# Weight casts issued ahead of group 0's masks, half transposes ahead of the context stores, the down tile's load behind a denominator hop

## The chip, the cores and the metric

The kernel runs on one core of one Trainium2 chip. The metric is the device time of one execution in microseconds (us), lower is better; the time before is the median of three runs.

## The reference

Two transformer layers over x of shape 1 x 1024 x 512. The part around the change is the first layer's attention and the weights that the later parts need:

```python
q = jnp.dot(x, Wq)                  # 32 query heads of 16
k, v = ...                          # 8 key/value heads; 4 query heads share one
scores = einsum('bhqd,bhkd->bhqk', q, k); scores = where(causal, -inf, scores)
ctx = softmax(scores / sqrt(16)) @ v
x = x + layernorm(ctx @ Wo + bo)
# L0 ffn: gate_t, up_t, down_t are int32 in {-1, 0, 1}, scaled by row
hidden = silu(x @ gate_w.T) * (x @ up_w.T); out = hidden @ down_w.T
# L1: mixing along D by autocorrelation (rfft, top 6 lags, softmax, rolled sums)
# L1 ffn: the same form with float weights w plus low-rank terms, w + b @ a
```

Every sublayer ends in a layernorm and a residual sum.

## The kernel before, in words

The program is written engine by engine, with semaphores set by hand; the order of each engine's work is the order of the code.

**Ahead of attention.** The projections are made and split in three bf16 pieces, which go out to `qp_d` and `kp_d` in DRAM. Beside them the low-rank products `b @ a` of the second ffn are made tile by tile (L1108), copied by ACT (L929), added by POOL to the loaded weight tile (`pool_lora`, L1050, 22 tiles) and stored by ACT's queue (L919).

**Attention in eight groups of four heads** (`for_groups`: group 0, a loop over groups 1 to 4, then groups 5, 6, 7 written out). For the eight key tiles kt of a group g, PE makes: row scores of a group ahead (L1533, plus the diagonal's mask L1536), of which DVE takes row maxima (L1418, L1420); transposed scores of g (L1546), which ACT exponentiates (L1506) and POOL masks on the diagonal (L1398); and the weighted sums (L1569). The row scores run `NT + LEAD` = 14 tiles ahead: from kt = 2 of group g they are those of group g + 2. Their queries lie in `qt6`, a ring of three, so the queries of group g + 2 may be loaded only when group g - 1 has used its own: `sp_group` waits for `st_ready` and then issues `load_q(sp, g + 2)` (L1307, six DMAs of 128 KB) at the very start of group g.

**SyncE's queue (SP)** issues nearly every DMA, in program order, and stands still at each wait. One group before the change: the queries' load; the down tile's load (L442, 688 KB, groups 1 to 4); then seven hops in the order of `HOPS`: "den" of the group before (denominators out L1328, back as 128 x 32 L1331, reciprocals out L1334, broadcast back L1338) and "max" of the next group (transpose L1314, out L1317, back L1320); then the context stores (L1346, four DMAs, which wait until POOL has normalised in L1389), the down tile's store (L447, which waits for DVE's sum L1131) and, in groups 1 to 4, `sp_weights0`: one DMA transpose of half of a weight (L432 for up, L434 for down). Group 0 is followed by the transpose of the whole gate weight (L432) and by `sp_early`, three small loads (L389 to L391).

**The casts.** gate_t, up_t and down_t are int32 in DRAM. Three DMAs of POOL's queue write them to DRAM as 16-bit numbers (`w16_d`); the gate's is issued near the start (L1676), those of up and down (L1407, L1408) at the end of POOL's part of group 0, behind its eight masks. `sp_weights0` waits for them (`w0_cast`).

The rest (output product, first ffn, mixing, second ffn) begins behind group 7 and is not touched.

Of the kernel before, what the change touches and what calls it, by code (L numbers as in the profile page):

```python
# [97 lines left out]
def build(nc, x_in, Wq, Wkv, Wo, bo, gate_t, up_t, down_t, gate_s, up_s, down_s,  # L98
          gate_w, up_w, down_w_in, gate_a, gate_b, up_a, up_b, down_a, down_b, dft, power, inverse, out):
    with ExitStack() as ctx:  # L100
# [337 lines left out]
        def down_row_load(sp, n):  # L438

            if n > 0:  # L440
                sp.wait_ge(down_stored, 16 * n)
            sp.dma_start(down_w, down_lora_w[n * P:(n + 1) * P, :]).then_inc(down_loaded, 16)  # L442
# [846 lines left out]
        def for_groups(eng, body):  # L1289

            body(eng, 0, 0)
            with eng.Fori(1, ND + 1) as g:
                body(eng, g, 1)
            body(eng, ND + 1, ND + 1)
            body(eng, G - 2, G - 2)
            body(eng, G - 1, G - 1)
# [48 lines left out]
                at = REP * HD * upper + HD * h  # L1345
                sp.dma_start(ctxt[at:at + HD, g - ND * upper, :], ctxn[32 * h:32 * h + HD, :]).then_inc(stored or ctx_stored, 16)  # L1346

        def sp_group(sp, g, shape, upper=0, w0=None):


            if shape < G - 2:

                if shape > 0:
                    sp.wait_ge(st_ready, 32 * g)
                else:
                    sp.wait_ge(qt_loaded, 2 * 16 * len(TERMS))
                load_q(sp, g + 2)
            if 1 <= g <= ND:
                down_row_load(sp, g - 1)
            for path, hop in HOPS:  # L1360
                if path == "den" and shape > 0:
                    den_hop(sp, g - 1, hop)
                if path == "max" and shape < G - 1:
                    maxima_hop(sp, g + 1, hop)
                if shape == G - 1 and (path, hop) == ("den", 1):
                    hidden_store(sp, 1, 5)
            if shape == G - 2:
                sp.wait_ge(st_ready, 32 * (G - 2))
                hidden_load(sp, 2)
                hidden_load(sp, 3)  # L1370
            if shape == G - 1:
                hidden_store(sp, 2, 6)
            if shape > 0:
                ctx_store(sp, g - 1, upper)
            if 1 <= g <= ND:
                down_row_store(sp, g - 1)
            if shape == G - 2:
                hidden_store(sp, 0, 4)
            if shape == G - 1:
                hidden_store(sp, 3, 7)  # L1380
            if w0 is not None:
                sp_weights0(sp, w0)

        def normalise(pool, g):

            pool.wait_ge(rec_loaded, 16 * REP * (g + 1))
# [4 lines left out]
        def pool_group(pool, g, shape):  # L1391

            for kt in range(NT):
                pool.wait_ge(p_ready, 32 * g + 4 * kt + 4)
                diag = probs[:, kt % 2, :, kt * P:(kt + 1) * P]
                pool.sem_inc(pool_passed)

                nc.gpsimd.affine_select(out=diag, in_=diag, compare_op=ALU.is_ge, fill=0.0, base=0,  # L1398
                                        pattern=[[0, REP], [1, P]], channel_multiplier=-1).then_inc(masked, 1)
                if kt == 0:  # L1400
                    if shape > 0:
                        pool.wait_ge(pv_done, NT * g)
                    nc.gpsimd.tensor_copy(vcur[:, :, 0:HD], vall[:, :, g, :]).then_inc(vcur_ready, 1)
                if kt == NORM_STEP and shape > 0:
                    normalise(pool, g - 1)
            if shape == 0:
                pool.dma_start(w16_d[1], up_t).then_inc(w0_cast[1], 16)  # L1407
                pool.dma_start(w16_d[2], down_t).then_inc(w0_cast[2], 16)  # L1408

        def row_max(dve, g, pos, before=None):  # L1410

# [189 lines left out]
        @block.sync  # L1601
        def _(sp):
            for half in range(2):
                sp.dma_start(x[:, 4 * half:4 * half + 4, :], x_in[0].rearrange("(t p) d -> p t d", p=P)[:, 4 * half:4 * half + 4, :]).then_inc(x_loaded[half], 16)
            sp.wait_ge(lora_clear, 1)
            sp_lora(sp)
            sp.dma_start(wkv, Wkv.rearrange("(c p) n -> p c n", p=P)).then_inc(wkv_loaded, 16)
            sp.dma_start(wq, Wq.rearrange("(c p) n -> p c n", p=P)).then_inc(wq_loaded, 16)
            sp_lora_stack(sp)

            for j in range(1 + ND):
                sp.wait_ge(pieces_ready, j + 1)
                for i in range(3):
                    dst = kp_d[i] if j == 0 else qp_d[i, (j - 1) * P:j * P, :]
                    sp.dma_start(dst, pc[i][:, j % 2, :]).then_inc(pieces_stored[j % 2], 16)
                if j == 0:
                    sp_lora_rows(sp)
                    sp.wait_ge(pieces_stored[0], 48)
                    for _, s, n in BLOCKS:
                        sp.dma_start(kt6[HD * s:HD * (s + n), :, :].rearrange("p g t -> p (g t)"),  # L1620
                                     kp_d[0:n].rearrange("a (d g) t -> (a d) (g t)", g=G)).then_inc(kt_loaded, 16)
                if j == 1:
                    sp.wait_ge(pieces_stored[1], 48)
                    load_q(sp, 0)
                    sp.wait_ge(qt_loaded, 16 * len(TERMS))
                    load_q(sp, 1)
            sp_lora_down(sp)
            for upper in range(2):
                half = slice(upper * D // 2, (upper + 1) * D // 2)
                sp.dma_start(wo[upper * P // 2:(upper + 1) * P // 2, :, :],  # L1630
                             Wo[half, :].rearrange("(c p) n -> p c n", p=P // 2)).then_inc(wo_loaded, 16)
            sp.wait_ge(pieces_stored[0], 48 * 3)
            sp.wait_ge(pieces_stored[1], 48 * 2)
            for hop in range(3):
                maxima_hop(sp, 0, hop)

            sp_group(sp, 0, 0, 0, 0)
            sp_early(sp)
            all_lora_stored(sp)
            for g, (i, n0, n1) in enumerate(((1, 0, N0 // 2), (1, N0 // 2, N0), (2, 0, N0 // 2), (2, N0 // 2, N0)), 1):  # L1640
                sp_group(sp, g, 1)
                sp_weights0(sp, i, n0, n1)
            sp_group(sp, ND + 1, 1, 1)
            sp_tables(sp)
            hidden_load(sp, 0)
            hidden_load(sp, 1)
            sp_group(sp, G - 2, G - 2, 1)
            sp_group(sp, G - 1, G - 1, 1)

            for hop in range(4):  # L1650
                den_hop(sp, G - 1, hop)
            ctx_store(sp, G - 1, 1, ctx_stored_last)
            hidden_store(sp, 4, 8)
            hidden_store(sp, 5, 9)
            hidden_store(sp, 6)
            hidden_store(sp, 7)
            sp_rest(sp)

        @block.gpsimd
        def _(pool):  # L1660
# [21 lines left out]
            pool.wait_ge(pool_chain, 4)  # L1682
            pool.wait_ge(v_ready, 1)
            pool_lora(pool)
            for_groups(pool, pool_group)
            normalise(pool, G - 1)
            pool_rest(pool)
# [226 lines left out]
```

## Time and profile before

| | |
|---|---|
| median of 3 runs | 857.82 us (856.72 to 858.96) |
| the profiled execution | 854.87 us, of which the span is 853.1 us |
| PE busy | 732.0 us (86%) |
| DVE, ACT, POOL busy | 618.8, 352.2, 281.4 us |
| mean share of the 16 DMA engines, queue 1 (SP's) | 40.3% |

How to read it: times count from the start of the span. PE is the matrix engine, DVE the vector engine, ACT the scalar engine. SPq and POOLq stand for the queues that issue DMAs; a DMA's time on SPq is its issue, and its landing is told apart. "[12.20 <-X]" is the idle time of the engine in front of a row, and what ended it.

### The profile page before, as it was taken

The numbers are of one execution on the slowest core, as the hardware profiler recorded it, in microseconds if no ns is written. First come the engines' busy times: TensorE is split into PE (matmuls) and PEld (weight loads), VectorE is DVE, ScalarE is ACT, GpSimd is POOL, SyncE is SP. The second block draws the span as 40 slices with busy tenths as digits, with TensorE's granted clock in tenths as the row PEclk, the third lists the DMA queues.
The fourth block names the chain that finished last, engine by engine and source line by source line (L and its number), as shares of the span: only waits on it lengthen the run. The fifth ranks groups of instructions, "written<-read, shape, count | busy, mean of one in ns | idle before, by whom it ended". The sixth has DMA issues, their size and how long they took to land.

```text
span 853.1 us, 15357 instructions
## 1 busy us (share of the span) xinstructions
PE 732.0 (86%) x5381; PEld 434.3 (51%) x5402; DVE 618.8 (73%) x1306; ACT 352.2 (41%) x683; POOL 281.4 (33%) x334
## 2 busy tenths in 40 slices
PE   0897889669989998978869998799989999899994
PEld 0552334223434333323337666576767777677772
DVE  6734996547676776785489999986977986786703
ACT  0232135436555565666004444345353443433231
POOL 4043321102212122133104555357535424244331
PEclk9998879969999999978989999799999999999998
DMA  8699845836283652454461479531584111110200
GB/s 207 214 212 299 246 113 92 184 103 124 67 160 83 136 108 51 116 140 129 106 178 26 105 110 226 135 73 68 102 146 64 26 38 27 25 50 1 51 26 25
DMA packets 140924, 93.65 MB, mean 110 GB/s; under 512 B 112024, under 2 KB 119064, under 8 KB 140552
## 3 DMA queue, kind: packets, MB, share of 16 engines
q1 hardware_dynamic: 134416, 76.09, 40.3%
q10 hardware_dynamic: 6208, 11.28, 4.2%
q0 software_dynamic: 240, 5.51, 3.2%
q8 instruction: 36, 0.59, 0.3%
q14 instruction: 24, 0.20, 0.1%
HBM read 48.73 MB, written 29.04 MB: 91 GB/s over the span
## 4 chain that ended last, share of the span: by engine, by line
PE 50%; DVE 22%; DMA 11%; SPq 5%; ACT 5%; issue 5%; POOL 3%; ACTq 0%; DVEq 0%; POOLq 0%
PE ps L1258 16%; PE ps L1280 8%; PE ps L1569 8%; DMA arena<-qp_d 6%; PE ps L1533 6%; DVE mx L1418 5%; PE ps L1546 5%; PE ps L1236 4%; PE ps L1794 2%; SPq L1307 2%; ACT arena L1506 2%; DMA arena<-in_L_attn_Wkv_dram 1%; DMA qp_d<-arena 1%; DVE mx L1420 1%; DVE rstd L253 1%
## 5 line engine op out<-in xcount | busy, mean ns | idle before, releaser
L1258 PE MATMUL ps<-arena 128*128 128x256 f16 (+1 forms) x1952 | 234.8, 277 | 6.7 <-DMA arena<-arena 6.6
L1258 PEld LDWEIGHTS ps<-arena 128*128 128x128 f16 (+1 forms) x1952 | 195.0, 101 | 49.4 <-issue 8.0
L1506 ACT ACTIVATE arena<-ps 128x1024 f32<-128x1024 f32 (+7 forms) x256 | 159.8, 651 | 124.7 <-PE ps L1546 120.7
L1418 DVE TENSOR_REDUCE mx<-ps 128x1 f32<-128x512 f32 (+1 forms) x256 | 156.2, 652 | 52.9 <-PE ps L1533 32.7
L1533 PE MATMUL ps<-arena 96*128 (+4 forms) x384 | 130.4, 354 | 39.6 <-DMA arena<-qp_d 20.9
L1087 POOL TENSOR_TENSOR arena<-arena 128x256 f32<-128x256 f32 (+1 forms) x100 | 82.2, 822 | 234.0 <-ACT arena L978 231.8
L1280 PE MATMUL ps<-arena 128*128 128x512 f16 (+2 forms) x467 | 117.9, 381 | 18.7 <-POOL arena L1093 17.3
L1546 PE MATMUL ps<-arena 99*128 (+4 forms) x384 | 124.3, 342 | 9.3 <-ACT arena L1506 7.7
L1398 POOL TENSOR_SCALAR_AFFINE_SELECT arena<-arena 128x512 f32<-128x512 f32 x64 | 41.9, 655 | 228.1 <-ACT arena L1506 228.1
L1533 PEld LDWEIGHTS ps<-arena 96*128 96x128 bf16 (+1 forms) x384 | 38.5, 101 | 125.6 <-issue 62.6
L1569 PE MATMUL ps<-arena 128*32 128x256 f32 (+1 forms) x1280 | 84.8, 373 | 4.6 <-POOL arena L1398 4.1
L1093 POOL TENSOR_TENSOR arena<-arena 128x256 f16<-128x256 f32 (+1 forms) x100 | 81.9, 819 | 0.0
L1280 PEld LDWEIGHTS ps<-arena 128*128 128x128 f16 (+1 forms) x488 | 45.7, 98 | 58.6 <-POOL arena L1093 22.1
L977 ACT ACTIVATE arena<-ps,gs 128x256 f32<-128x256 f32 (+1 forms) x44 | 20.9, 474 | 115.0 <-PE ps L1258 115.0
L977 ACT ACTIVATE arena<-ps,sc 128x256 f32<-128x256 f32 x56 | 26.6, 474 | 87.5 <-PE ps L1258 87.5
L1546 PEld LDWEIGHTS ps<-arena 99*128 (+1 forms) x384 | 36.3, 99 | 50.6 <-ACT arena L1506 19.9
L1536 PE MATMUL ps<-arena 128*128 128x128 bf16 x256 | 57.3, 230 | 0.0
L1420 DVE TENSOR_REDUCE mx<-ps 128x2 f32<-128x512 f32 (+1 forms) x48 | 32.8, 689 | 31.7 <-PE ps L1536 31.3
L1236 PE MATMUL ps<-arena 128*128 128x256 f16 (+1 forms) x384 | 47.5, 283 | 6.9 <-POOL arena L1069 5.7
L1050 POOL TENSOR_TENSOR arena<-arena 128x512 f32<-128x512 f32 (+1 forms) x22 | 29.4, 1348 | 71.6 <-ACT arena L929 71.6
L1569 PEld LDWEIGHTS ps<-arena 128*32 128x32 f32 x1280 | 32.2, 110 | 38.0 <-issue 16.5
L1236 PEld LDWEIGHTS ps<-arena 128*128 128x128 f16 x384 | 38.4, 101 | 17.1 <-POOL arena L1069 6.5
(160 smaller groups left out, 837.9 us busy)
## 6 DMA issues: line engine op xcount, KB each, us to landing
arena<-qp_d SPq DMA_DIRECT2D x48, 128.0 KB, 5.0
lora_d<-arena ACTq DMA_DIRECT2D x20, 256.0 KB, 6.2
arena<-lora_d SPq DMA_DIRECT2D x10, 512.0 KB, 5.1
w1n_d<-arena SPq DMA_DIRECT2D x10, 512.0 KB, 3.5
arena<-rec_d SPq DMA_DIRECT2D x32, 128.0 KB, 2.7
qp_d<-arena SPq DMA_DIRECT2D x12, 256.0 KB, 7.6
w1dn_d<-arena SPq DMA_DIRECT2D x4, 704.0 KB, 4.5
arena<-in_L_ffn_down_w_dram SPq DMA_DIRECT2D x4, 688.0 KB, 7.4
```

The lines of the kernel that those rows point to most:

```text
L977: nc.scalar.activation(sg[0:h, b, :], ps[0:h, b, 0:CH], ACT.Silu, scale=gate[0:h, ht:ht + 1]).then_inc(sg_ready, 1)
L1087: nc.gpsimd.tensor_tensor(hs[0:h, b, :], sg[0:h, b, :], u_sb[0:h, b, :], ALU.mult).then_inc(hs_ready, 1)
L1093: nc.gpsimd.tensor_tensor(hid[0:h, 1, b, :], hs[0:h, b, :], hid[0:h, 0, b, :], ALU.subtract).then_inc(hid_ready, 1)
L1236: last = nc.tensor.matmul(to, lhs(w, kt), rhs(r, kt), start=(kt, w, r) == (parts[0], 0, 0), stop=(kt, w, r) == (parts[-1], 1, 0))
L1258: last = nc.tensor.matmul(ps[0:h, b, CH * o:CH * (o + 1)], w(t[0])[:, kt, ht * P:ht * P + h], xt[:, c, t[1], kt, :], start=(kt, t) == (0, ...
L1280: last = nc.tensor.matmul(ps[:, y_bank(k, i), :], hid[0:h, t[0], b, i * P:(i + 1) * P], down[0:h, ht, :], start=ht == 0 and t == terms[0], ...
L1418: nc.vector.reduce_max(to[:, h, t:t + 1], s_bank(g, u)[:, 0:w], mybir.AxisListType.X).then_inc(s_taken, 1)
L1506: nc.scalar.activation(probs[:, kt % 2, h, kt * P:T], st_bank(h).rearrange("p b n -> p (b n)")[:, kt * P:T], ACT.Exp, scale=HD ** -0.5).th ...
L1533: last = nc.tensor.matmul(to, qt6[0:QROWS, g % RING, heads[i], qt * P:(qt + 1) * P], kt6[0:QROWS, g, k0:k1], start=True, stop=not diagonal)
L1536: last = nc.tensor.matmul(to[:, w - P:w], ident16[:, :], strip[:, :], start=False, stop=True)
L1546: last = nc.tensor.matmul(st_bank(h)[:, b, q0 - b * 512:512], kt6[0:QROWS + MROWS, g, kt * P:(kt + 1) * P], qt6[0:QROWS + MROWS, g % RING, ...
L1569: last = nc.tensor.matmul(o_bank[32 * h:32 * h + 32, b, q0 - b * 512:q1 - b * 512], vcur[:, kt, :], probs[:, kt % 2, h, q0:q1], start=kt = ...
```

## The change

It does three things, and removes or adds no instruction.

1. The casts of up and down leave the end of group 0 on POOL and stand directly behind `pool_lora`, ahead of group 0.
2. In `sp_group` the call of `sp_weights0` moves from behind the stores to the place ahead of `ctx_store`. For group 0, which has no stores, this changes nothing.
3. `down_row_load` moves from ahead of the hops to behind the hop ("den", 1).

```diff
--- before.py
+++ after.py
@@ -1345,7 +1345,7 @@
                 at = REP * HD * upper + HD * h
                 sp.dma_start(ctxt[at:at + HD, g - ND * upper, :], ctxn[32 * h:32 * h + HD, :]).then_inc(stored or ctx_stored, 16)
 
-        def sp_group(sp, g, shape, upper=0, w0=None):
+        def sp_group(sp, g, shape, upper=0, w0=()):
 
 
             if shape < G - 2:
@@ -1355,13 +1355,13 @@
                 else:
                     sp.wait_ge(qt_loaded, 2 * 16 * len(TERMS))
                 load_q(sp, g + 2)
-            if 1 <= g <= ND:
-                down_row_load(sp, g - 1)
             for path, hop in HOPS:
                 if path == "den" and shape > 0:
                     den_hop(sp, g - 1, hop)
                 if path == "max" and shape < G - 1:
                     maxima_hop(sp, g + 1, hop)
+                if (path, hop) == ("den", 1) and 1 <= g <= ND:
+                    down_row_load(sp, g - 1)
                 if shape == G - 1 and (path, hop) == ("den", 1):
                     hidden_store(sp, 1, 5)
             if shape == G - 2:
@@ -1370,6 +1370,8 @@
                 hidden_load(sp, 3)
             if shape == G - 1:
                 hidden_store(sp, 2, 6)
+            if w0:
+                sp_weights0(sp, *w0)
             if shape > 0:
                 ctx_store(sp, g - 1, upper)
             if 1 <= g <= ND:
@@ -1378,9 +1380,6 @@
                 hidden_store(sp, 0, 4)
             if shape == G - 1:
                 hidden_store(sp, 3, 7)
-            if w0 is not None:
-                sp_weights0(sp, w0)
-
         def normalise(pool, g):
 
             pool.wait_ge(rec_loaded, 16 * REP * (g + 1))
@@ -1403,9 +1402,6 @@
                     nc.gpsimd.tensor_copy(vcur[:, :, 0:HD], vall[:, :, g, :]).then_inc(vcur_ready, 1)
                 if kt == NORM_STEP and shape > 0:
                     normalise(pool, g - 1)
-            if shape == 0:
-                pool.dma_start(w16_d[1], up_t).then_inc(w0_cast[1], 16)
-                pool.dma_start(w16_d[2], down_t).then_inc(w0_cast[2], 16)
 
         def row_max(dve, g, pos, before=None):
 
@@ -1634,12 +1630,11 @@
             for hop in range(3):
                 maxima_hop(sp, 0, hop)
 
-            sp_group(sp, 0, 0, 0, 0)
+            sp_group(sp, 0, 0, 0, (0, 0, N0))
             sp_early(sp)
             all_lora_stored(sp)
             for g, (i, n0, n1) in enumerate(((1, 0, N0 // 2), (1, N0 // 2, N0), (2, 0, N0 // 2), (2, N0 // 2, N0)), 1):
-                sp_group(sp, g, 1)
-                sp_weights0(sp, i, n0, n1)
+                sp_group(sp, g, 1, 0, (i, n0, n1))
             sp_group(sp, ND + 1, 1, 1)
             sp_tables(sp)
             hidden_load(sp, 0)
@@ -1682,6 +1677,8 @@
             pool.wait_ge(pool_chain, 4)
             pool.wait_ge(v_ready, 1)
             pool_lora(pool)
+            pool.dma_start(w16_d[1], up_t).then_inc(w0_cast[1], 16)
+            pool.dma_start(w16_d[2], down_t).then_inc(w0_cast[2], 16)
             for_groups(pool, pool_group)
             normalise(pool, G - 1)
             pool_rest(pool)
```

POOL, where the low-rank sums (L1050) end and group 0 begins; L1398 and L1397 are the masks, L1403 and L1402 the copy of the values:

```order
 L1050 TENSOR_TENSOR arena<-arena 96x512
-L1398 AFFINE_SELECT arena<-arena 128x4x128
-L1403 COPY arena<-arena 128x8x16
-L1398 AFFINE_SELECT arena<-arena 128x4x128 x7
-L1407 DMA w0u_d<-in_L_ffn_up_t_dram 64x14336
-L1408 DMA w0d_d<-in_L_ffn_down_t_dram 64x14336
+L1680 DMA w0u_d<-in_L_ffn_up_t_dram 64x14336
+L1681 DMA w0d_d<-in_L_ffn_down_t_dram 64x14336
+L1397 AFFINE_SELECT arena<-arena 128x4x128
+L1402 COPY arena<-arena 128x8x16
+L1397 AFFINE_SELECT arena<-arena 128x4x128 x7
 L1292 UNCONDITIONAL_BRANCH
```

Both casts have moved ahead of all eight masks of group 0; the loop over groups 1 to 4 begins at L1292.

SP at the start of a group (1 to 4 alike), from the queries' load to the reciprocals' store:

```order
 L1307 DMA arena<-qp_d 16x4x1024 x6
-L442 DMA arena<-in_L_ffn_down_w_dram 128x1376
 L1328 DMA den_d<-arena 4x1024
 L1331 DMA dens<-den_d 128x32
+L442 DMA arena<-in_L_ffn_down_w_dram 128x1376
 L1314 DMA_TRANSPOSE mt<-m 128x128
 L1334 DMA rec_d<-recs 128x32
```

The down tile's load now follows the two hops that bring the denominators out and back.

SP at the end of a group, from the broadcast of the reciprocals to the next group's query load:

```order
 L1338 DMA arena<-rec_d 32x1024 x4
 L1320 DMA arena<-mt_d 3x4096
+L432 DMA_TRANSPOSE arena<-w0u_d 128x4x896
 L1346 DMA arena<-arena 16x1024 x4
 L447 DMA lorad_d<-arena 128x1376
-L432 DMA_TRANSPOSE arena<-w0u_d 128x4x896
 L1307 DMA arena<-qp_d 16x4x1024 x6
```

The half transpose has moved ahead of the context stores (L1346) and the down tile's store (L447), and nothing stands between that store and the next query load.

## Rows read from the trace of the kernel before

**Rows 1.** The page, parts 1 and 4: busy time; last chain by line.

```profile
PE 732.0 (86%) x5381; PEld 434.3 (51%) x5402; DVE 618.8 (73%) x1306; ACT 352.2 (41%) x683; POOL 281.4 (33%) x334
...
PE ps L1258 16%; PE ps L1280 8%; PE ps L1569 8%; DMA arena<-qp_d 6%; PE ps L1533 6%; DVE mx L1418 5%; PE ps L1546 5%; PE ps L1236 4%; PE ps L1794 2%; SPq L1307 2%; ACT arena L1506 2%; DMA arena<-in_L_attn_Wkv_dram 1%; DMA qp_d<-arena 1%; DVE mx L1420 1%; DVE rstd L253 1%
```

**Rows 2.** PE's waits, 150 to 360 us: total, times, longest.

```profile
PE ps L1533 <- DMA arena<-qp_d: 16.7, 5, 12.2
PE ps L1533 <- DVE mx L1418: 4.0, 15, 0.4
```

**Rows 3.** PE's timeline, groups 1, 2, 3, 5: start, length, [idle before].

```profile
177.11 0.61 PE L1533 MATMUL ps<-arena 96*128 x1 [12.20 <-DMA arena<-qp_d]
...
215.79 0.39 PE L1533 MATMUL ps<-arena 96*128 x1 [0.91 <-DMA arena<-qp_d]
...
251.72 0.39 PE L1533 MATMUL ps<-arena 96*128 x1 [0.66 <-DMA arena<-qp_d]
...
324.46 0.39 PE L1533 MATMUL ps<-arena 96*128 96x512 bf16 x1 [2.23 <-DMA arena<-qp_d]
```

**Rows 4.** Stretches: length, busy of each engine, PEclk, DMA share, GB/s.

```profile
121.00:134.00 13.00, 12.41 (x95) 4.36 (x93) 11.38 (x25) 8.97 (x10) 1.51 (x3) 1.00 0.00 0
...
165.00:177.00 12.00, 0.00 (x0) 0.00 (x0) 0.00 (x0) 0.00 (x0) 0.64 (x1) 0.57 0.93 225
177.00:182.00 5.00, 4.89 (x28) 2.07 (x28) 3.04 (x8) 1.62 (x2) 0.00 (x0) 0.50 0.05 15
```

**Rows 5.** DMA: POOL's queue, whole run; cast and down tile, 150 to 160.

```profile
q0 software_dynamic: 240, 5.51, 3.2%
...
w0d_d<-in_L_ffn_down_t_dram POOLq DMA_DIRECT2D x1, 1792.0 KB, 20.8
...
arena<-in_L_ffn_down_w_dram SPq DMA_DIRECT2D x1, 688.0 KB, 20.9
```

**Rows 6.** L1307: landing of the six query loads, groups 1, 2, 0.

```profile
DMA to landing us min/median/max: 3.2/16.9/20.0
...
DMA to landing us min/median/max: 3.6/5.0/6.1
...
DMA to landing us min/median/max: 2.7/4.6/5.2
```

**Rows 7.** POOL's timeline: last sum, group 0's first mask, first moved cast.

```profile
117.48 1.26 POOL L1050 TENSOR_TENSOR arena<-arena 96x512 f32<-96x512 f32 x1 [1.93 <-ACT arena L929]
125.59 0.64 POOL L1398 TENSOR_SCALAR_AFFINE_SELECT arena<-arena 128x512 f32<-128x512 f32 x1 [6.85 <-ACT arena L1506]
...
153.84 0.54 POOL L1407 DMA_DIRECT2D w0u_d<-in_L_ffn_up_t_dram  x1
```

**Rows 8.** SP's timeline, group 0 into group 1: start, length.

```profile
134.25 1.13 SPq L1314 DMA_TRANSPOSE mt<-m  x1
...
138.31 7.21 SPq L432 DMA_TRANSPOSE arena<-w0g_d  x1
...
147.14 1.46 SPq L391 DMA_DIRECT2D row_b<-in_L_attn_bo_dram  x1
152.89 4.26 SPq L1307 DMA_DIRECT2D arena<-qp_d  x6
```

**Rows 9.** SP's timeline, end of group 1; last transpose of group 4.

```profile
188.31 0.30 SPq L1320 DMA_DIRECT2D arena<-mt_d  x1
197.27 2.51 SPq L1346 DMA_DIRECT2D arena<-arena  x4
201.31 0.35 SPq L447 DMA_DIRECT2D lorad_d<-arena  x1
201.70 5.00 SPq L432 DMA_TRANSPOSE arena<-w0u_d  x1
206.75 2.93 SPq L1307 DMA_DIRECT2D arena<-qp_d  x6
...
309.67 6.54 SPq L434 DMA_TRANSPOSE arena<-w0d_d  x1
```

## The prediction

> **What bounds the kernel now.** I read the page first. PE is busy 86% of the span and heads the chain of work that ended last, but one entry among the first lines of that chain is no engine: the load of queries from `qp_d`, 6% of the span [rows 1]. A transfer in the chain means that PE stood and waited for it. So I read PE's waits in the attention groups: the row scores (L1533) wait 16.7 us for that load, in five places, one of them 12.2 us long; next to that all waits for DVE's maxima are fifteen tiny ones, 4.0 us in all [rows 2]. PE's timeline places them: 12.20 us before 177.11 (group 1), 0.91 before 215.79 (group 2), 0.66 before 251.72 (group 3) and 2.23 before 324.46 (group 5) [rows 3]. What is left of the 16.7 is 0.7, group 4. The reader should see one stop per group, always at the same matmul: the first row score of group g + 2, whose queries SP could ask for only at the start of group g.
>
> Why is the load late? Two reasons, and they differ.
>
> In group 1 SP issues it in time, at 152.89 [rows 8], but the six parts need up to 20.0 us to land, against at most 6.1 us in group 2 and 5.2 us in group 0 [rows 6]. What is different is that POOL issues the two casts 0.95 us later, at 153.84 [rows 7]; the second lands 20.8 us after its issue, and the down tile's load behind the queries takes 20.9 us too [rows 5]. The DMA engines are 93% busy through the stop [rows 4]. At the stop no compute engine works except one mask.
>
> In groups 2 to 5 the load lands normally but is issued late. The stop of group 1 begins at 177.11 - 12.20 = 164.91, which is 12.0 us after the issue at 152.89. In group 2 it begins at 215.79 - 0.91 = 214.88, so that group began near 202.9, yet SP issues the load only at 206.75, straight from a half transpose that held its queue from 201.70 for 5.00 us [rows 9]. SP is 3.9 us late there. In group 5 it is later still: the transpose at 309.67 takes 6.54 us [rows 9], and that is where the wait is 2.23 us.
>
> **The change part by part.**
>
> *The casts.* Nothing is added; the two DMAs start behind the last low-rank sum, at 117.48 + 1.26 = 118.7 instead of 153.84 [rows 7]. Their queue moved all three casts with 3.2% of the 16 engines' span, 27.3 us [rows 5], so two are 18.2 us of all engines. In place the pair took 0.54 + 20.8 = 21.3 us from the first issue to the last landing, among other traffic. I take the longer, so they end by 140.0. From 121 to 134 the engines move nothing (share 0.00) while PE is 95% busy at full clock [rows 4]. That is the cover. The casts go from DRAM to DRAM, so no compute engine waits for them. On POOL the two issues cost 0.54 us each, and POOL's next work is the mask at 125.59, in front of which it idles 6.85 us [rows 7]. What could be hit in their new place: group 0's own query load, whose issues end at 113.6 and whose last part takes at most 5.2 us [rows 6], so it has landed before 119; and the maxima's hops, which SP starts at 134.25 [rows 8]. These three small transfers may hang until the casts end, 140.0 instead of 136.6 for the first. Then the gate transpose moves from 138.31 to at most 141.8, and `sp_early`, which ended at 147.14 + 1.46 = 148.6, to 152.1. SP waits there until 152.89 anyway, so nothing is passed on. In group 1 the load then takes what it takes in group 2: 2.93 us of issue (206.75) and all landed when PE goes on, 215.79 - 206.75 = 9.0 us. PE asks for it after 12.0. The stop of 12.20 us goes whole.
>
> With it goes a slow stretch. The stop lets the granted clock fall to 0.50, 1.2 instead of 2.4 GHz, and from 177 to 182 PE is 98% busy at 0.50 [rows 4]: 5 us for 2.5 us of work. From resuming in group 1 to resuming in group 2 are 38.68 us, from there to group 3 are 35.93; the difference of 2.75, less that of the two stops (0.25), is 2.5 again. I take **2.5 us**.
>
> *The half transposes.* Between L1320, issued by 188.6, and the context stores at 197.27 SP does nothing for 8.7 us; it waits for POOL's normalisation [rows 9]. A transpose of 5.00 us fits, and so does the longest, 6.54. Then the stores (2.51), the wait for DVE's sum, the down tile's store at 201.31, and SP is free at 201.7, ahead of the group's end near 202.9. The query load goes out on time and lands 9.0 us later, 3 us before it is wanted. The same holds for groups 3 to 5, whose stops come at the same point, 35.9 us apart [rows 3]. All four short stops go: 0.91 + 0.66 + 0.7 + 2.23 = **4.5 us**. The transposes' DMA work no longer runs ahead of the query load in SP's queue but in a stretch where only the reciprocals' loads are before it.
>
> *The down tile's load.* It moves past two hops of 16 KB. It was issued right behind the queries, at 206.75 + 2.93 = 209.7, 6.8 us into the group. Two hops, each with a landing to wait for, come ahead of it now; three like hops took 138.31 - 134.25 = 4.1 us [rows 8], so it starts near 11 us into the group. Queries of 768 KB land in 9.0, so its 688 KB are there by 20, and DVE adds to them only from step 5 of 8, 22 us in. The cost is between nothing and the few us by which it may hold up the maxima's transpose behind it; SP's 8.7 us of idle ahead of the stores, less 5.0 for the half transpose, takes up 3.7 of them. I take 0. It may even help the denominators by as much, and nobody waits for these.
>
> *Given back.* With the stops gone, DVE's small waits behind them have less cover: fifteen cost 4.0 us, 0.27 each [rows 2]. Two more of them make **0.5 us** (an estimate; between 0 and the 4.5 us of the short stops).
>
> **The sum.** 12.2 + 2.5 + 4.5 - 0.5 = 18.7 us. The profiled execution took 854.87, so it would take 836.2. It lies 2.95 us below the median of the runs, 857.82, and I set the same gain against the median: **839.1**, as 839. Nothing after group 7 is touched, and it is timed by semaphores, so I expect the gain to arrive whole at the end.
>
> **Where the skill says otherwise.** The wait of group 1 rests on one reading, that the casts alone made the query load slow. It had at most 6.1 us without them, and got 20.0 with them [rows 6]. So the row gives the casts the whole of the delay. The Trainium skill, "DMA: Bandwidth & Descriptors", section "Queues, rings and completion order", says that each DMA engine takes turns between the queues it has work for, a whole packet of some 9 to 17 descriptors at a time. By that the load should have slipped in between a few cast packets and lost far less than it did, and the gain of the change would be that of rival B, 11 us. The row disagrees with it, and I go by the row.
>
> **The rivals.**
>
> A, the forecast: 0.76. 836 to 842.
>
> B, the casts did only part of it: 0.07. Suppose the load fits between cast packets and loses three of them. The 240 packets of the casts' queue take 27.3 x 16 / 240 = 1.8 us each [rows 5], so it would have landed at 152.89 + 9.0 + 5.5 = 167.4, and the other 9.7 us to 177.11 come from something that stays (the down tile's load, the first turn of the loop). A load that lands without the casts at 171.6 still stops PE for 6.7 us. Gain 5.5 + 4.5 + perhaps 1 = 11: **847**. This is what the page's turn-taking would make of it. Against: group 2 has the same down tile behind it and lands in 9.0.
>
> C, the casts run longer in the new place and reach into SP's chain: 0.08. The first hop landed at 136.6, and the gate transpose and three loads filled SP to 148.6, 12.0 us later; with 9.0 of landing the queries come at T + 21, T being the casts' end. PE stands from T = 144 on. At T = 150 the stop is 6 us and the gain about 12: **846**. They would have to take 31 us instead of 21.3.
>
> D, slower: 0.03. The same mechanism carried on: the stop of before is back at T = 156, and the 4.5 us of the short stops are used up near T = 161. From there each us of the casts is a us lost. At T = 170, **867**. That asks for 42 us or more, twice the duration measured. For it speaks only that the first small transfer behind the casts in group 1 also hung; against it, the empty stretch from 121 to 134 and no other traffic to share with.
>
> E, the change does nothing that counts: 0.04. The 12.2 us come from the loop's first turn, and the order on SP just moves its lateness (the transpose shares the engines with the context stores, normalisation comes later, the load is late again): **857**. Against: the first stop begins at the same point as the others, 12 us into the group.
>
> F, more than the forecast, 0.02: PE's clock holds in other stretches too.
>
> **How the numbers follow.** The predicted time is A's. The range takes in A and the centres of B and C: 835 to 849. About 0.3% (2.6 us) is what a measurement of this kernel can tell from no change. Faster by more than that: A, B, C and F, 0.93. Within: 0.04, E. Slower: 0.03, D.
>
> **What would show it.** In the profile after, PE's waits for `qp_d` in the groups should fall from 16.7 us to under 1; the DMA engines should be busy from 119 to about 140 and the query load of group 1 land in some 6 us; no stretch at half clock near 180; SP should issue each query load some 12 us before its matmul, with the half transposes standing where it idled. I am wrong if PE stops near 165 again, if it waits at a group's start for the maxima (hops stuck behind the casts), or if the stops turn into waits for DVE of the same length.

## The result and the profile after

The changed kernel takes 837.57 us in the median of four runs (835.81 to 838.58), the kernel before 858.39 beside it. The ratio is 0.9756, with an interval of 0.9729 to 0.9782: 20.8 us less by the medians, between 18.7 and 23.3 by the interval. Run again in the last set of experiments, on another occasion, the same kernel gave 839.78 against 858.27, ratio 0.9795 (0.976 to 0.983), 18.5 us less by the medians and 17.6 by the ratio. The forecast was 839.

The profiled execution took 838.06 us, with a span of 836.3. Its page, parts 1 and 4, against [rows 1]:

```profile
PE 732.5 (88%) x5402; PEld 434.2 (52%) x5402; DVE 620.6 (74%) x1306; ACT 352.1 (42%) x683; POOL 283.6 (34%) x334
...
PE ps L1258 16%; PE ps L1565 9%; PE ps L1280 8%; PE ps L1529 6%; DVE mx L1414 6%; PE ps L1542 5%; PE ps L1236 5%; DMA qp_d<-arena 2%; ACT arena L1502 2%; DVE mx L1416 1%; DMA arena<-in_L_attn_Wkv_dram 1%; POOL arena L1397 1%; PE ps L1532 1%; DVE rstd L253 1%; PE ps L1791 1%
```

PE does the same work in a shorter span, and the load of queries has gone from the front of the chain. Lines up to 1347 keep their numbers; behind them the row scores are L1529 (L1533 before), the transposed ones L1542, the masks L1397, and the casts L1680 and L1681.

PE's waits from 118 to 345 us, against [rows 2] (total, times, longest):

```profile
PE ps L1529 <- DVE mx L1414: 5.0, 18, 0.4
PE ps L1529 <- DVE mx L1416: 2.8, 7, 1.7
```

No wait for `qp_d` is left in the groups. Those for DVE's maxima are what they were in the same stretch before (4.7 us in 18 and 2.8 us in 7 waits), small and many.

SP's timeline, group 0 into group 1, and the groups' query loads, against [rows 8, 9] (start, length):

```profile
136.06 4.66 SPq L1314 DMA_TRANSPOSE mt<-m  x1
143.73 0.34 SPq L1317 DMA_DIRECT2D mt_d<-mt  x1
...
145.50 6.88 SPq L432 DMA_TRANSPOSE arena<-w0g_d  x1
...
153.98 1.35 SPq L391 DMA_DIRECT2D row_b<-in_L_attn_bo_dram  x1
155.59 3.85 SPq L1307 DMA_DIRECT2D arena<-qp_d  x6
...
175.69 4.01 SPq L432 DMA_TRANSPOSE arena<-w0u_d  x1
184.31 2.51 SPq L1346 DMA_DIRECT2D arena<-arena  x4
188.29 0.34 SPq L447 DMA_DIRECT2D lorad_d<-arena  x1
189.44 2.76 SPq L1307 DMA_DIRECT2D arena<-qp_d  x6
```

Two things are to be seen. The half transpose at 175.69 fills the idle time ahead of the context stores at 184.31, and SP now waits 0.8 us for the group's end before the load at 189.44, instead of coming 3.9 us late. And the maxima's transpose of group 0, issued at 136.06, comes back only at 143.73, 7.7 us later instead of 2.3. The casts ran beside it, as POOL's timeline and the DMA view from 119 to 125 show:

```profile
120.49 0.52 POOL L1680 DMA_DIRECT2D w0u_d<-in_L_ffn_up_t_dram  x1
121.01 0.50 POOL L1681 DMA_DIRECT2D w0d_d<-in_L_ffn_down_t_dram  x1
```

```profile
w0u_d<-in_L_ffn_up_t_dram POOLq DMA_DIRECT2D x1, 1792.0 KB, 12.6
w0d_d<-in_L_ffn_down_t_dram POOLq DMA_DIRECT2D x1, 1792.0 KB, 20.9
```

They start at 120.49 and end at 121.01 + 20.9 = 141.9. The two stretches of [rows 4] to compare, the one that now holds the casts, and the one that ran at half clock:

```profile
119.00:140.00 21.00, 18.23 (x142) 6.90 (x140) 17.82 (x35) 11.82 (x14) 4.36 (x7) 1.00 0.99 222
...
177.00:182.00 5.00, 4.84 (x49) 2.14 (x45) 3.60 (x6) 2.97 (x6) 1.32 (x3) 1.00 0.91 188
```

The DMA engines are full from 119 to 140 with PE at full clock, and PEclk is 1.00 from 177 to 182.

**Where the 16.8 us between the two spans lie.** Take two marks of the same work: POOL's last mask of group 0 (153.26 before, 155.07 after) and SP's denominators out in group 6 (L1328, 351.35 and 333.40). Between them lay 198.1 us and lie 178.3: 19.8 less. Ahead of the first mark this execution is 1.8 us longer and behind the second 1.2 us, in stretches whose instructions are the same. This execution issues group 0's query load at 112.72, 1.8 us later than the one before (110.92), and nothing ahead of that is changed. The experiments' profiles start it anywhere between 110.47 and 113.33, so I take these 3 us as scatter between executions.

A third mark comes once in every group: POOL's copy of the values, behind the group's first mask. From group to group it takes 49.93, 36.18, 35.85, 35.56 and 36.08 us before (groups 1 to 5) and 35.08, 35.10, 35.12, 34.77 and 33.78 after. So group 1 is 14.9 us shorter, groups 2 to 4 are 1.1, 0.7 and 0.8 shorter, and group 5 is 2.3 shorter.

### The profile page after: what moved, and what is told of

Read it like the earlier page. It is cut to its first block, busy times and chain, and to the rows that moved or that the text cites. A ratio compares the mean times of both kernels' runs of the same rounds, so it can differ in the third digit from the quotient of the medians.

```text
span 836.3 us, 15378 instructions
## 1 busy us (share of the span) xinstructions
PE 732.5 (88%) x5402; PEld 434.2 (52%) x5402; DVE 620.6 (74%) x1306; ACT 352.1 (42%) x683; POOL 283.6 (34%) x334
## 4 chain that ended last, share of the span: by engine, by line
PE 52%; DVE 23%; DMA 7%; ACT 6%; issue 5%; POOL 4%; SPq 3%; ACTq 0%; DVEq 0%; POOLq 0%
PE ps L1258 16%; PE ps L1565 9%; PE ps L1280 8%; PE ps L1529 6%; DVE mx L1414 6%; PE ps L1542 5%; PE ps L1236 5%; DMA qp_d<-arena 2%; ACT arena L1502 2%; DVE mx L1416 1%; DMA arena<-in_L_attn_Wkv_dram 1%; POOL arena L1397 1%; PE ps L1532 1%; DVE rstd L253 1%; PE ps L1791 1%
## 5 line engine op out<-in xcount | busy, mean ns | idle before, releaser
L1414 DVE TENSOR_REDUCE mx<-ps 128x1 f32<-128x512 f32 (+1 forms) x256 | 156.2, 652 | 33.0 <-PE ps L1532 18.7
L1529 PE MATMUL ps<-arena 96*128 (+4 forms) x384 | 129.4, 352 | 23.5 <-DVE mx L1414 7.2
L1280 PE MATMUL ps<-arena 128*128 128x512 f16 (+2 forms) x488 | 122.8, 382 | 18.2 <-POOL arena L1093 18.1
L1542 PE MATMUL ps<-arena 99*128 (+4 forms) x384 | 122.5, 336 | 9.3 <-ACT arena L1502 7.7
L1397 POOL TENSOR_SCALAR_AFFINE_SELECT arena<-arena 128x512 f32<-128x512 f32 x64 | 41.8, 654 | 207.8 <-ACT arena L1502 207.8
L1529 PEld LDWEIGHTS ps<-arena 96*128 96x128 bf16 (+1 forms) x384 | 38.5, 100 | 109.3 <-issue 48.7
L1093 POOL TENSOR_TENSOR arena<-arena 128x256 f16<-128x256 f32 (+1 forms) x100 | 83.8, 839 | 0.0
L977 ACT ACTIVATE arena<-ps,gs 128x256 f32<-128x256 f32 (+1 forms) x44 | 20.8, 474 | 116.5 <-PE ps L1258 116.5
L1542 PEld LDWEIGHTS ps<-arena 99*128 (+1 forms) x384 | 35.9, 98 | 49.5 <-ACT arena L1502 19.9
L1050 POOL TENSOR_TENSOR arena<-arena 128x512 f32<-128x512 f32 (+1 forms) x22 | 29.0, 1328 | 74.0 <-ACT arena L929 74.0
L1565 PEld LDWEIGHTS ps<-arena 128*32 128x32 f32 x1280 | 32.0, 109 | 37.1 <-issue 15.5
L1236 PEld LDWEIGHTS ps<-arena 128*128 128x128 f16 x384 | 38.3, 101 | 16.8 <-POOL arena L1069 6.5
```

Of the source, the lines that this page charges most:

```text
L1093: nc.gpsimd.tensor_tensor(hid[0:h, 1, b, :], hs[0:h, b, :], hid[0:h, 0, b, :], ALU.subtract).then_inc(hid_ready, 1)
L1236: last = nc.tensor.matmul(to, lhs(w, kt), rhs(r, kt), start=(kt, w, r) == (parts[0], 0, 0), stop=(kt, w, r) == (parts[-1], 1, 0))
L1280: last = nc.tensor.matmul(ps[:, y_bank(k, i), :], hid[0:h, t[0], b, i * P:(i + 1) * P], down[0:h, ht, :], start=ht == 0 and t == terms[0], ...
L1414: nc.vector.reduce_max(to[:, h, t:t + 1], s_bank(g, u)[:, 0:w], mybir.AxisListType.X).then_inc(s_taken, 1)
L1529: last = nc.tensor.matmul(to, qt6[0:QROWS, g % RING, heads[i], qt * P:(qt + 1) * P], kt6[0:QROWS, g, k0:k1], start=True, stop=not diagonal)
L1542: last = nc.tensor.matmul(st_bank(h)[:, b, q0 - b * 512:512], kt6[0:QROWS + MROWS, g, kt * P:(kt + 1) * P], qt6[0:QROWS + MROWS, g % RING, ...
```

## The experiments

Each is compared with the kernel before, run on the same chip in the same set: 856.0 us in the first set, 856.6 in the second, 858.3 in the third. The us gained are differences of medians. The ratios are not exactly the quotients of these medians, and their intervals reach 3 to 4 us to either side, so single microseconds are read from the traces and not from the times.

**The three parts, one by one.** Part 1 alone: the two cast lines moved behind `pool_lora(pool)`.

```diff
-            if shape == 0:
-                pool.dma_start(w16_d[1], up_t).then_inc(w0_cast[1], 16)
-                pool.dma_start(w16_d[2], down_t).then_inc(w0_cast[2], 16)
...
             pool_lora(pool)
+            pool.dma_start(w16_d[1], up_t).then_inc(w0_cast[1], 16)
+            pool.dma_start(w16_d[2], down_t).then_inc(w0_cast[2], 16)
```

> Part 1 alone: both casts behind the last low-rank sum, SP's order as before. My theory (the casts starve group 1's query load, SP's lateness makes the four short stops): the stop of 12.2 us and the half-clock stretch (2.5 us) go, the four short stops (0.9, 0.7, 0.7, 2.2) stay. Time 858.4 - 14.7 = 843.7, PE's waits for qp_d in the groups 4 to 5 us. Rival E (the stop belongs to the first turn of the loop): the stop stays and the time is within 3 us of 858.4. Rival B (casts only part of it): a stop of some 6 us stays, 852.

Measured: 841.03 us, ratio 0.9812 (0.9778 to 0.9846), 15.0 us less by the medians, 13.2 to 19.0 by the interval. PE's waits in the groups, and the last of the short stops:

```profile
PE ps L1530 <- DMA arena<-qp_d: 3.0, 4, 0.8
```

```profile
309.20 0.39 PE L1530 MATMUL ps<-arena 96*128 96x512 bf16 x1 [0.77 <-DMA arena<-qp_d]
```

POOL's copies of the values, which open groups 1 and 2, in the kernel before and in this one:

```profile
160.31 0.29 POOL L1403 COPY arena<-arena 128x128 f32 x1
210.24 0.29 POOL L1403 COPY arena<-arena 128x128 f32 x1
...
161.41 0.29 POOL L1403 COPY arena<-arena 128x128 f32 x1
196.48 0.29 POOL L1403 COPY arena<-arena 128x128 f32 x1
```

The stop of 12.2 us is gone and the four short ones stand. Group 1 takes 35.07 us in place of 49.93, 14.9 less, which is the stop and 2.7 us more. So the long stop was the casts' doing, not the first turn of the loop, and not partly something else. But the short stops are 3.0 us together, not 4.5: the one of group 5 is 0.77, where the profile before had 2.23 [rows 3].

Part 2 alone, in `sp_group`:

```diff
             if shape == G - 1:
                 hidden_store(sp, 2, 6)
+            if w0:
+                sp_weights0(sp, *w0)
             if shape > 0:
                 ctx_store(sp, g - 1, upper)
...
-            if w0 is not None:
-                sp_weights0(sp, w0)
```

> Part 2 alone: the half transposes ahead of the context stores, casts and down tile's load as before. My theory: the stop of 12.2 us stays, the four short stops go; 858.4 - 4.5 = 853.9, and SP issues the query loads of groups 2 to 5 at the groups' start, some 3.9 us earlier in the group. Rival (a transpose that shares the engines with the loads around it delays normalisation, context stores and the next load): the short stops stay, 858.

Measured: 852.89 us, ratio 0.9953 (0.9923 to 0.9983), 3.1 us less. Waits of PE, and SP's timeline of the end of group 1:

```profile
PE ps L1532 <- DMA arena<-qp_d: 12.2, 1, 12.2
```

```profile
190.72 3.67 SPq L432 DMA_TRANSPOSE arena<-w0u_d  x1
199.32 2.52 SPq L1346 DMA_DIRECT2D arena<-arena  x4
...
204.51 2.77 SPq L1307 DMA_DIRECT2D arena<-qp_d  x6
```

Only the long stop is left; the query load goes out 5.2 us after the context stores began, against 9.5 before [rows 9]. The context stores are not late for the transpose, which issues in 3.67 us here: they begin 11.78 us after the maxima's hop (L1317) in this kernel and in the one before.

Part 3 alone:

```diff
-            if 1 <= g <= ND:
-                down_row_load(sp, g - 1)
             for path, hop in HOPS:
...
+                if (path, hop) == ("den", 1) and 1 <= g <= ND:
+                    down_row_load(sp, g - 1)
```

> Part 3 alone: the down tile's load behind the hop den 1. My theory: worth nothing, 858.4 within 1.5, all five stops as before; in group 1 the denominators' hop hangs behind the queries under the casts as before. Rival (the down tile's 688 KB share the engines with the query load, so moving them away lets it land earlier): the query load of groups 2 to 5 lands 1 us or more earlier and the short stops of 0.7 and 0.9 go, 856; in group 1 it lands several us earlier too.

Measured: 855.16 us, ratio 0.9987 (0.9956 to 1.0018), 0.8 us less, not to be told from none. The long stop stays and so do three short ones, 2.2 us together; group 4, which stopped for 0.73 us before, has none here:

```profile
PE ps L1533 <- DMA arena<-qp_d: 14.8, 4, 12.6
```

The query loads of groups 2 to 5 land in at most 6.0, 6.2, 5.7 and 5.6 us, against 6.1 in group 2 before [rows 6]. The load lands no earlier with the down tile out of its way. That the short stops are 2.2 us and not 4.5 is mostly group 5 again, 0.82 for 2.23, and 1.4 us are left to groups 2 to 4, against 2.2 and 2.3 in part 1 alone and in the kernel before. Whether part 3 is worth the 0.9 us between them, one execution does not tell.

Parts 1 and 2 without part 3:

> Parts 1 and 2 without part 3: the down tile's load right behind the queries as before. My theory: part 3 is worth nothing, so the time is that of the whole change, 837.6 within 1.5, and PE does not wait for qp_d in the groups. Rival (the down tile beside the query load counts): the query load lands later than in the whole change by 1 us or more, but it has 3 us in hand, so a small stop at most and under 1 us of time.

Measured: 837.27 us, ratio 0.978 (0.9742 to 0.9819), 18.7 us less, and PE has no wait for `qp_d` in the groups. That is the whole change as far as the intervals tell (15.5 to 22.1 here); 15.0 and 3.1 make 18.1.

**Casts twice as long in the new place.** The mechanism of the rivals C and D, brought about on purpose:

```diff
             pool.dma_start(w16_d[2], down_t).then_inc(w0_cast[2], 16)
+            pool.dma_start(again_d[0], up_t).then_inc(again, 16)
+            pool.dma_start(again_d[1], down_t).then_inc(again, 16)
```

Left out here are the two DRAM tensors, their semaphore and a wait for it at the end of POOL's program.

> The whole change, with both casts issued a second time (into other DRAM tensors) right behind the first, so that the casts run twice as long in the new place. In the profile of the whole change they ended at 141.9, the first maxima hop issued at 136.06 landed at 143.73 with them, the query load of group 1 was issued at 155.59 and landed in 8. Mechanism of my rivals C and D (small transfers of SP's queue hang until the casts end): the casts end near 163, the hop lands near 164, PE waits some 13 us at the start of group 1 for the maxima and some 5 us more for the queries, with the half clock behind it 858 to 862. Against it (the queues take turns packet by packet): each hop loses 2 to 4 us, PE waits little, 838 to 843.

Measured: 852.02 us, ratio 0.9944 (0.9913 to 0.9974). Of the 18.7 us some 14 are gone. The last cast, issued at 120.01, landed 37.4 us later, at 157.4. SP's and PE's timelines:

```profile
135.04 1.13 SPq L1316 DMA_TRANSPOSE mt<-m  x1
157.06 0.34 SPq L1319 DMA_DIRECT2D mt_d<-mt  x1
...
169.24 2.96 SPq L1309 DMA_DIRECT2D arena<-qp_d  x6
```

```profile
161.56 0.61 PE L1531 MATMUL ps<-arena 96*128 x1 [7.99 <-DMA arena<-mt_d]
...
178.06 0.61 PE L1531 MATMUL ps<-arena 96*128 x1 [2.45 <-DMA arena<-qp_d]
```

The maxima's transpose, issued at 135.04, comes back at 157.06, with the end of the casts: 22 us for 32 KB. PE then stands 7.99 us at the start of group 1 for the maxima, and 2.45 us more for the queries. The granted clock falls behind both, to 0.50 from 160 to 165 and to 0.54 from 180 to 185. From mark to mark groups 0 and 1 take 43.75 and 40.54 us against 34.13 and 35.08 in the whole change, 15.1 us more, of which the two stops are 10.4. The time is 6 us below what I wrote, because the casts ended at 157.4 and not at 163: the two more took 17 us and not 21, and this execution began them 2 us earlier.

That the transpose hung to the end of the casts was no rule of "held back until they end". The DMA view from 141 to 143 us, packets in the first column:

```profile
q0 software_dynamic: 15, 0.43, 99.9%
...
q1 hardware_dynamic: 16, 0.00, 1.6%
```

In these 2 us each of the 16 DMA engines moves about one packet of the casts (q0) and one of SP's queue (q1). It is so all the way from 139 to 157 us, 12 to 26 packets of each in every 2 us, and those of SP's queue come to 160 in all. The same transpose in the kernel before is 160 packets too (134 to 136.6 us), ten per engine. So a small transfer does take turns with the casts, and ten turns, most of them behind a packet of some 2 us, make the 18 us. What falls is the rival's price of 2 to 4 us, which counted one or two turns where there were ten. That the ten turns and the casts ran out together was chance.

**One cast in the old place, one in the new.**

```diff
                 pool.dma_start(w16_d[1], up_t).then_inc(w0_cast[1], 16)
-                pool.dma_start(w16_d[2], down_t).then_inc(w0_cast[2], 16)
...
             pool_lora(pool)
+            pool.dma_start(w16_d[2], down_t).then_inc(w0_cast[2], 16)
```

> The kernel before with the down cast in the new place and the up cast alone in the old one. My theory (the query load of group 1 lands when the casts issued beside it end): the cast takes 10.5 us, ends near 164.5 and the queries land near 166; PE asks at 164.9, so a stop of 1 to 2 us remains and the clock stays up: 856 - 12 - 1.5 = 842.5. Rival E (first turn of the loop) keeps 12 us. A rival in which the stop depends on any cast traffic and not its length keeps most of it, 850 or more.

Measured: 848.29 us, ratio 0.9894 (0.9843 to 0.9945), 8.3 us less; 842.5 was expected. The cast was issued at 157.32 and landed 12.2 us later, at 169.5. PE's timeline where it goes on in group 1, then in groups 2 and 3:

```profile
172.24 0.61 PE L1532 MATMUL ps<-arena 96*128 x1 [3.85 <-DMA arena<-qp_d]
```

```profile
210.42 0.39 PE L1532 MATMUL ps<-arena 96*128 x1 [0.50 <-DMA arena<-qp_d]
```

```profile
246.32 0.39 PE L1532 MATMUL ps<-arena 96*128 x1 [0.64 <-DMA arena<-qp_d]
```

And the stretches around the stop (PEclk is the third number from the end):

```profile
165.00:170.00 5.00, 3.34 (x40) 1.23 (x32) 2.24 (x6) 1.91 (x3) 0.64 (x1) 1.00 0.86 193
170.00:175.00 5.00, 2.76 (x11) 1.33 (x12) 1.67 (x5) 0.81 (x1) 0.00 (x0) 0.67 0.51 144
175.00:180.00 5.00, 5.00 (x43) 1.94 (x41) 2.90 (x7) 2.11 (x3) 0.00 (x0) 0.64 0.05 10
180.00:185.00 5.00, 4.47 (x49) 1.74 (x41) 2.66 (x5) 2.33 (x4) 0.64 (x1) 1.00 0.46 120
```

The length of the casts sets the stop, as the theory says, but the stop is 3.85 us: the cast took 12.2 us and not 10.5, and the queries landed 2.7 us after it and not 1.5. What I had wrong besides is the clock. It falls for this short stop too, to 0.67 and 0.64, and costs as much as behind the long one: resume to resume is 38.18 us from group 1 to 2 and 35.90 to group 3, a loss of 2.3, and 2.4 with the difference of the stops.

**The same bytes in short rows, in the old place.** Why do 18 us of casts hold back a load on another queue to the end? Each packet of the casts is long: 1.8 us by the sums of [rows 5]. The DMA view of the kernel before from 170 to 172 us, inside the long stop, has this for the casts' queue and for SP's:

```profile
q0 software_dynamic: 16, 0.46, 106.5%
q1 hardware_dynamic: 16, 0.03, 4.8%
```

Again it is one packet of either per engine in 2 us, and so it is in each 2 us from 160 to 172, apart from one in which it is two and two. The 16 packets of the casts carry 0.46 MB, so each is one row of 14336 16-bit numbers, and takes 2.1 us (106.5% of 2 us); the 1.8 us are a mean over these and some that carry next to nothing. SP's packets here move 2 KB. The query load of 768 KB is then 384 of them, 24 per engine, against eight rows per engine of the two casts (64 rows a cast). Some ten per engine had passed by 158, when the long packets filled the engines; from there on the load moved on by one short packet per long one until the casts were through.

If so, short packets should let it pass. This kernel cuts each cast in two by columns, so that its DMAs consist of rows of 256 or 896 numbers instead of 14336.

```diff
-                pool.dma_start(w16_d[1], up_t).then_inc(w0_cast[1], 16)
+                for k in range(2):
+                    a, b = k * D // 2, (k + 1) * D // 2
+                    pool.dma_start(w16_d[1][:, a:b], up_t[:, a:b]).then_inc(w0_cast[1], 16)
```

The down cast is cut likewise, and `sp_weights0` waits for both halves.

> The kernel before, casts in their old place, but each cut in two by columns, so that its DMAs are made of rows of 256 (up) or 896 (down) numbers in place of 14336. The same bytes. If the queries hang because each turn of a DMA engine on the casts' queue is one long packet (about 2 us), shorter pieces let the load of group 1 land in 6 to 12 us instead of 20, the stop of 12.2 us falls below 4 and the time is 843 to 848. If SP's transfers hang behind the casts whatever their packets, or share by bytes, the stop stays above 8 us and the time within 4 of 856; if the shorter rows make the casts themselves slower, it may be longer than before.

Measured: 841.0 us, ratio 0.9821 (0.9775 to 0.9867), 15.6 us less, as much as moving them, and PE has no stop in group 1. The page's line of the casts' queue, the DMA view from 150 to 160 us, and the landing of group 1's six query loads:

```profile
q0 software_dynamic: 4752, 5.51, 4.0%
...
w0u_d<-in_L_ffn_up_t_dram POOLq DMA_DIRECT2D x2, 896.0 KB, 13.6
w0d_d<-in_L_ffn_down_t_dram POOLq DMA_DIRECT2D x2, 896.0 KB, 21.4
arena<-qp_d SPq DMA_DIRECT2D x6, 128.0 KB, 4.1
arena<-in_L_ffn_down_w_dram SPq DMA_DIRECT2D x1, 688.0 KB, 7.9
```

```profile
DMA to landing us min/median/max: 3.0/4.1/6.2
```

The queue's packets are 4752 where they were 240, 0.11 us each by the same sum (4.0% of the 16 engines' span of 837.3 us). The casts themselves take no less than before (21.4 us is the median of the down halves), and the queries still land in at most 6.2 us beside them, where it was 20.0 [rows 6]. The whole bytes are the same, so it is not the casts' bytes as such that stopped the load but the length of the pieces. (The casts are also four DMAs here and not two, and from 150 to 160 us they moved 0.53 MB where the long ones moved 0.92; no run tells these apart from the length itself. Nor are the turns one for one among short packets: from 158 to 160 us it is 577 of the casts' and 102 of SP's.) This is what the Trainium skill, "DMA: Bandwidth & Descriptors", section "Queues, rings and completion order", says of turns taken packet by packet; my reading of it as a few lost turns left out that the load itself is 24 packets per engine.

**Short rows with the rest of the change.** Three kernels in one set: the whole change; parts 2 and 3 with the cut casts in the old place; and the whole change with cut casts.

> The whole change once more, beside the next two on one chip. 0.976 of the time before, as measured; 837 to 838.

> Parts 2 and 3 of the change, with the casts in their old place but cut by columns (short rows). If the long packets alone made the casts harmful, the place no longer matters: no stop at the query load of group 1, no half-clock stretch, and the time of the whole change within 2 us. If the place still counts (the casts share the engines with the load, the down tile and the hops), a stop of some us in group 1 or a wait at a later group's start, 840 or more.

> The whole change with the casts cut by columns. The first maxima hop of group 0 no longer hangs (2.3 us to land in place of 7.7) and SP is free some 5 us before group 1 begins; PE did not wait there before, so the time is that of the whole change within 1.5 us. If something in group 0 or 1 did wait on the late hop, up to 1 us less.

| kernel | median, us | ratio | interval |
|---|---|---|---|
| whole change | 839.78 | 0.9795 | 0.976 to 0.983 |
| parts 2, 3, cut casts in the old place | 837.01 | 0.9753 | 0.9721 to 0.9786 |
| whole change with cut casts | 835.71 | 0.975 | 0.9715 to 0.9786 |

None of the three waits for `qp_d` in the groups. The intervals overlap, so no order among the three is shown. The 4 us between the first and the last are not settled: their profiled executions took 835.65 and 835.4, and their groups 1 to 5 differ by 0.1 us at most. With short rows the place of the casts makes no difference that the times show. The trace shows a small one: in the second kernel group 1 takes 36.41 us against 35.07 in the first. The maxima's transpose, issued at 170.71 beside the casts, is back only at 176.99, and POOL waits 2.78 us for the reciprocals that come behind it. The transpose of group 0's maxima, issued at 135.38 in the third kernel, was back at 141.11, 5.7 us and not the 2.3 I expected:

```profile
135.38 1.13 SPq L1314 DMA_TRANSPOSE mt<-m  x1
141.11 0.34 SPq L1317 DMA_DIRECT2D mt_d<-mt  x1
```

So short rows do not free a DMA transpose from the casts' company as they free the plain loads. Here turns of one for one do not explain it: from 135.3 to 141.2 us its 160 packets stand beside 610 of the casts. Why, no run here tells; PE does not wait for it.

## Why the prediction was right, step by step

*The long stop, 12.2 us, from the casts.* Right, and whole. Rival E fell with part 1 alone (no stop at all) and with it rival B.

*The half-clock stretch, 2.5 us.* Right: group 1 alone is 14.9 us shorter with part 1, against 12.2 + 2.5 = 14.7, and the kernel with one cast shows the cost apart, 2.4 us behind a stop of 3.85.

*The short stops, 4.5 us.* The mechanism was right, the size too high. They came from one execution, in which the last half transpose took 6.54 us and the stop behind it 2.23. In the profiles of parts 1 and 3 alone and of the single cast in the old place that stop is 0.77, 0.82 and 0.98, with transposes of 4.65 to 4.71 us; in the one with cut casts 1.74, with 6.07. The four stops sum to 3.0 in part 1 alone, to 2.2, 2.9 and 3.6 in the other three and to 4.5 before, and part 2 alone gains 3.1. So the term should have been 3.0.

*The down tile's load, 0.* Right: 0.8 us alone, with no change within its interval, and nothing that shows is missing without it (837.27).

*Given back, 0.5.* Nothing was: between the marks groups 2 to 5 became shorter by 1.1, 0.7, 0.8 and 2.3 us, for stops of 0.91, 0.66, 0.73 and 2.23. With the measured sizes the sum is 12.2 + 2.5 + 3.0 = 17.7 against the 18.7 forecast. The two errors point opposite ways and leave 1 us. The measured gains, 20.8 and 18.5 for the whole change and 18.7 without part 3, scatter by more than that, so that 839 came within 1.5 us of 837.57 is in part luck.

*The new place is free.* Right for the time, but with less in hand than was worked out. The casts ended at 141.9, within 2 us of the estimate, 140.0. The first hop came back 1.8 us after them, and the gate transpose, put at 141.8 at the latest, was issued at 145.50. SP finished `sp_early` at 155.3 and not at 152.1, and came to group 1's query load at 155.59. By the last mask of group 0 this execution runs 1.8 us late, so that is 1 us of real lateness, out of 3 us in hand; "nothing is passed on" was too strong. The doubled casts show what the place costs when they last: the formula T + 21 of rival C gives 178.4 for their T of 157.4, and the queries came at 178.06. The hop ahead of it, though, was bound by its ten turns and not by the casts' end, so the formula is shown for this T and not for longer casts.

*The turns that the Trainium skill tells of.* I set the row against the rule, and by the rule made rival B, a load that loses three turns of 1.8 us. What failed there is the three, which came from no row. The traces show the turns themselves, one packet for one packet, and a load of 24 packets per engine that still had more than half of them to go at 158. Rule and row agree once the packets are counted. Going by the row was right, but the reason given, that the row disagrees with the rule, was not.

## What to carry to other kernels

A stop for a DMA that was issued in time asks what else is in the DMA engines; a large cast with rows of tens of kilobytes held back SP's transfers here, because each packet of theirs waited about 2 us for one of the cast. So count the packets per engine on both sides: the loss was about one long packet for each short one, as long as the long ones lasted. Both cures were cheap: issue the cast where nobody waits for a transfer, or cut its rows. On a queue that issues in order, put long issues where the queue already waits for an engine, ahead of that wait and not behind it. And take the size of a small stop from several groups or executions, not from the longest one.

## What the runs showed of the hardware that was not expected

- Beside a queue of long packets another queue gets one short packet per long one on each of the 16 DMA engines: 16 packets of the casts and 16 of SP's queue from 170 to 172 us before, although the former carry 28.7 KB each and the latter 2 KB; 15 and 16 from 141 to 143 with the doubled casts.
- A stop of PE of 3.85 us cost the same in clock as one of 12.2 us: 2.4 and 2.5 us of lost work. With the doubled casts a stop of 2.45 us, 14 us after a longer one, was followed by PEclk 0.54 from 180 to 185, and its group was 5.5 us longer than in the whole change, 3.0 more than the stop.
- The issue of the same half transpose takes 3.5 to 4.1 us in its new place, where loads of 128 KB and less went before it, and 4.6 to 6.5 us behind the down tile's store of 688 KB. The 32 KB transpose of the maxima takes 1.1 us to issue in group 0 of the kernel before, and 4.7 to 5.5 us in four profiles in which it is issued into the casts' last 6 us; with the doubled casts it was issued in 1.1 and came back after 22.
- Casts from DRAM to DRAM of 1.8 MB of output each: two end after 21 to 22 us, four after 39 us, with rows of 14336 numbers; with rows of 256 and 896 in the old place the last half landed 23.5 us after its issue, beside other loads.
